# A shorter pause in a gather pipeline: GpSimd waits for three tiles of a quad, the fourth tile counts on a semaphore of its own

## The reference

```python
# network 0, three layers
agg = segment_sum(e_w[:, None] * h[src], dst)            # gather by src, sum by dst
h = layernorm(relu(agg / sum_w @ w_neigh.T + h @ w_root.T + b))
# network 1
ef = (relu(edge_attr @ We1 + be1) @ We2 + be2) * sigmoid(ts @ Wt + bt)
msg = relu(concat([x[row], ef]) @ Wn1 + bn1) @ Wn2 + bn2
x = x + segment_sum(msg, col)
# network 2, two layers: a matrix for each of 8 edge types
x = segment_sum(xt[src, etype8], dst) + x @ Wl + b
# network 3, two layers: 8 heads, 32 edge types
a = (kw[src, etype32] * q[dst]).sum(-1) * pri;  att = edge_softmax(a, dst)
h = segment_sum(v[src, etype32] * att, dst) ...
```

## Time and profile before

| | us |
|---|---|
| median of 3 runs | 6471.04 (6457.61 to 6473.24) |
| profiled execution, own time | 6410.16 |
| its span | 6408.1 |
| GpSimd busy in the span | 3221.9 (50%) |
| of that the gathers, line 479, 3128 of them | 3001.8 |
| TensorE matmul busy | 3293.9 (51%) |
| VectorE busy | 2162.9 (34%) |
| ScalarE busy | 1006.4 (16%) |
| mean granted TensorE clock | 0.652 of full speed |

### The profile page before, as it was taken

How to read it: one execution, slowest core, us unless ns; L and a number is a source line. 1 busy time by engine, 2 the same in 40 slices (tenths; PEclk the granted TensorE clock), 3 DMA queues, 4 the chain that set the end, 5 groups by cost and what they waited for, 6 DMA issues and landing times. The chain is left out here.

```text
span 6408.1 us, 51881 instructions
## 1 busy us (share of the span) xinstructions
PE 3293.9 (51%) x13857; PEld 2295.6 (36%) x13857; DVE 2162.9 (34%) x5075; ACT 1006.4 (16%) x2209; POOL 3221.9 (50%) x3406
## 2 busy tenths in 40 slices
PE   5554677767774555643463344643324356333263
PEld 3333455545552333332343232233324322333153
DVE  3222322232224222411121114533338544333485
ACT  0000322232222111200010002400004324000063
POOL 4665466546663666366646663046650320566403
PEclk7676777677776777755565556755557677555586
DMA  2111334333432332211131116976653579766453
GB/s 61 46 47 40 88 98 101 98 82 99 101 99 79 91 90 82 107 46 47 46 131 47 46 46 251 427 239 185 182 149 111 149 287 427 204 187 184 118 148 95
DMA packets 630965, 826.34 MB, mean 129 GB/s; under 512 B 93075, under 2 KB 510341, under 8 KB 618133
## 3 DMA queue, kind: packets, MB, share of 16 engines
q1 hardware_dynamic: 480117, 492.37, 22.9%
q0 software_dynamic: 120608, 276.12, 16.2%
q10 hardware_dynamic: 29952, 54.54, 2.9%
HBM read 470.63 MB, written 352.04 MB: 128 GB/s over the span
## 5 line engine op out<-in xcount | busy, mean ns | idle before, releaser
L479 POOL DMA_INDIRECT arena<-table,idx_s x3128 | 3001.8, 960 | 2353.5 <-issue 1095.5
L751 PE MATMUL ps<-arena,work 128*128 x4160 | 985.9, 378 | 1050.0 <-issue 934.9
L751 PEld LDWEIGHTS ps<-arena,work 128*128 128x128 f32 x4160 | 824.8, 274 | 1317.4 <-issue 1170.3
L1965 PE MATMUL ps<-arena,work 128*128 x1664 | 412.7, 426 | 693.7 <-issue 488.2
L1965 PEld LDWEIGHTS ps<-arena,work 128*128 128x128 f32 x1664 | 359.1, 317 | 748.6 <-issue 530.1
L459 DVE TENSOR_SCALAR work<-iota_row,dl_s,w_s 128x128 f32<-128x128 f32 x1248 | 350.4, 358 | 454.6 <-issue 349.4
L455 DVE TENSOR_TENSOR work<-ps,dl_s 128x512 f32<-128x512 f32 x208 | 143.8, 692 | 926.5 <-issue 617.0
L1934 DVE TENSOR_TENSOR arena<-arena,ps 128x128 f32<-128x128 f32 x832 | 182.7, 281 | 741.9 <-issue 500.0
L929 DVE SCALAR_TENSOR_TENSOR arena<-ps,vecs,arena 128x256 f32<-128x256 f32 x208 | 100.6, 484 | 893.9 <-issue 435.9
L1832 PE MATMUL ps<-arena,work 32*128 32x512 f32 x1600 | 299.1, 876 | 97.5 <-DVE work L1859 44.2
L510 PE MATMUL ps<-work,picks 128*104 128x512 f32 x416 | 313.4, 842 | 46.2 <-issue 42.8
(11 more groups left out here) (331 smaller groups left out, 3539.5 us busy)
## 6 DMA issues: line engine op xcount, KB each, us to landing
table<-arena SPq DMA_DIRECT2D x96, 2048.0 KB
onehot<-col_rows ACTq DMA_DIRECT2D x208, 256.0 KB
values<-arena SPq DMA_DIRECT2D x832, 64.0 KB
arena<-values SPq DMA_DIRECT2D x208, 256.0 KB
arena<-table,idx_s POOLq DMA_INDIRECT x3128
arena<-edge_times SPq DMA_DIRECT2D x208, 128.0 KB
edge_part<-arena SPq DMA_DIRECT2D x208, 128.0 KB
table<-arena SPq DMA_DIRECT2D x50, 512.0 KB
```

The costliest lines, as they stand in the source:

```text
L479: pool.indirect_dma_start(ring[:, ds(t % RING * 2 * H, width)], None, tab, bass.IndirectOffsetOnAxis(ap=idx_s[:, t:t + 1], axis=0)).then_i ...
L751: mm = pe.matmul(accf[:, ds(b, P)], o, arena[:, ds(slot, H)], start=False, stop=False, skip_group_check=True)
L1965: mm = pe.matmul(ps[:, n % 8, c * P:(c + 1) * P], across_ring[:, n % DEEP, c * P:(c + 1) * P], Qn_flat[:, ds(b, P)], start=True, stop=True)
```

## The change

`gathers` gets a second set of 16 semaphores, `fourth`. The fourth tile of a quad adds its 16 there, the other three add to `gathered` as before. `hand_over(k)` waits for 48 on the one and for 16 on the other. After each quad the quad before it is handed over, now always and only that one. Each `rest`-th quad GpSimd then waits for the three first tiles of the quad just issued, without a hand-over.

```diff
             def hand_over(k):
-                pool.wait_ge(gathered[k % U].sem, gathered[k % U].at(64 * (k // U) + 16 * min(4, EDGE_TILES - 4 * k)))
+                pool.wait_ge(gathered[k % U].sem, gathered[k % U].at(48 * (k // U) + 16 * min(3, EDGE_TILES - 4 * k)))
+                if 4 * k + 3 < EDGE_TILES:
+                    pool.wait_ge(fourth[k % U].sem, fourth[k % U].at(16 * (k // U) + 16))
...
                 pool.indirect_dma_start(ring[:, ds(t % RING * 2 * H, width)], None, tab,
-                                        bass.IndirectOffsetOnAxis(ap=idx_s[:, t:t + 1], axis=0)).then_inc(gathered[t // 4 % U].sem, 16)
+                                        bass.IndirectOffsetOnAxis(ap=idx_s[:, t:t + 1], axis=0)).then_inc((fourth if t % 4 == 3 else gathered)[t // 4 % U].sem, 16)
                 if t % 4 == 3:
-                    done = t // 4 + 1
-                    for k in range(handed[0], done if done % rest == 0 else done - 1):
-                        hand_over(k)
-                        handed[0] = k + 1
+                    k = t // 4
+                    if k > 0:
+                        hand_over(k - 1)
+                        handed[0] = k
+                    if (k + 1) % rest == 0:
+                        pool.wait_ge(gathered[k % U].sem, gathered[k % U].at(48 * (k // U) + 48))
             for k in range(handed[0], TILE_QUADS):
                 hand_over(k)
```

More of the change, by code:

```diff
@@ L182, in build @@
         gathered = [signal(f"gathered{u}") for u in range(U)]
+        fourth = [signal(f"fourth{u}") for u in range(U)]
         arrived = signal("arrived")
@@ L556, in gather_pass_over @@
             for k in range(TILE_QUADS):
-                gathered[k % U].base += 16 * min(4, EDGE_TILES - 4 * k)
+                gathered[k % U].base += 16 * min(3, EDGE_TILES - 4 * k)
+                fourth[k % U].base += 16 * (4 * k + 3 < EDGE_TILES)
         def fill_rows(pe, row):
@@ L1972, in score_phase @@
                 for q in range(TILE_QUADS):
-                    gathered[q % U].base += 16 * min(4, EDGE_TILES - 4 * q)
+                    gathered[q % U].base += 16 * min(3, EDGE_TILES - 4 * q)
+                    fourth[q % U].base += 16 * (4 * q + 3 < EDGE_TILES)
                 for s in row_in:
```

## The result

The changed kernel takes 6614.65 us (median of 4 runs, 6606.82 to 6622.54) against 6464.32 us (4 runs, 6445.94 to 6473.24) of the kernel before: ratio 1.0236, 95% interval 1.0209 to 1.0264. It is 150 us slower, where 253 us less were forecast.

What follows compares the result with a forecast made beforehand. GpSimd's row of gathers and rests was taken to bound 4580 of 6408 us. Savings of 96 (P2, P3), 75 (P1, P5, P6), 30 (P4) and 52 (P7, P8) sum to 253: 6471 - 253 = 6218 us, range 6150 to 6450.

Steps and rivals of the forecast that it cites:

- The view of the bound: GpSimd's gathers and rests set the length of all eight gather passes, 4580 of 6408 us.
- The 10 to 17 us over the rests: GpSimd's idle in P1, P4, P5 and P6 beyond its pace and rests, put down to waits for a full ring.
- those with one every 20 do: Argument for the rival: passes with a rest every 20 us show ring waits, those with one every 10 us none.
- the term 3 x (30 - 5) = 75 us: P1, P5, P6: 30 us saved at rests in each, less 5 for ring waits in TensorE's slow stretches; bounds 0 and 90.
- P2 and P3: 96 us gained was forecast: Consumer chain at 5.3 us a step makes each pass 551 us, 48 gained in place of 60; bounds 0 and 60.
- P4, P7 and P8: 82 us gained was forecast: Shorter rests save 30 us in P4 and 52 in P7 and P8 together, 1.1 at each of their rests.
- The size of a rest: Waiting for the third tile ends each of 240 rests 1.25 us earlier, 2.34 to 1.09: 300 us at GpSimd.
- The later hand-over: Quads at rests are handed over some 4 us later; taken as nothing, or 32 us if its cover goes.
- The Trainium skill's rule: DMA engines alternate queues by whole packets; if half the saving were lost, P7 and P8 give 30 us, not 52.
- The rival: TensorE's slow stretches come to P2 and P3, 152 us longer for both; net 70 slower, 6541 us, chance 0.17.
- in P1 rests don't stop a crawl either: Argument against the rival: one of TensorE's slow stretches in P1 has two rests inside it.

Runs made afterwards that it cites:

- The run with the full rest: Changed kernel with GpSimd also waiting for the fourth tile at each rest, hand-over still one quad late: 6481.52 us, ratio 1.0022 to the kernel before.
- the last set of runs: Kernel before with no rests and evenly paced gathers (1.53, 1.44 or 1.39 us by pass) in all passes: 6360.03 us against 6318.55 for the kernel before.

## Why the prediction was wrong

**The view of the bound failed.** The sentence "a pass lasts as long as GpSimd's row of gathers and rests" took the rests for the reason of the row's length. In P1, P5 and P6 they are not: P1's row was 553.5 us with full rests, 557.5 with short ones, 554.0 with none, and 558.7 at 1.31 us. There the consumers set the row already, at the speed that the gathers leave TensorE; GpSimd sets P1's only when it is slower still (575.6 us at 1.44, 592.1 with a full rest at every second quad). The 10 to 17 us over the rests, which I counted as a side matter, were this bound showing. (P4 doesn't belong in that list: 55.6 - 49 is 6.6 us, and it has no ring waits, so "those with one every 20 do" was misread too.) So the term 3 x (30 - 5) = 75 us failed, and the larger one of P2 and P3 below. I took a loss of 5 us in each of P1, P5 and P6 for the ring; it was all of the gain and more. GpSimd's idle over its pace ahead of quads that are no rest went from 12.1 to 32.2 us in P1, from 6.0 to 47.3 in P5 and from 10.9 to 44.9 in P6, against 15.3, 39.1 and 33.5 us that the rests themselves gave (50.5 to 35.2, 55.8 to 16.7, 50.5 to 17.0; P1's rests still hold ring waits).

**P2 and P3: 96 us gained was forecast, 98 lost was measured.** The chain was sized at 5.3 us from its free run of 4.97. That run was itself one under full rests. With the gathers denser the median step did fall, from 5.54 to 5.16 us, but 18 steps of P2 take 8 us and more, up to 43.7, where none did before, as TensorE's word to ScalarE comes up to 20 us late. The bounds, 0 to 60 us of gain, left out that the price of a step depends on GpSimd's rate.

**P4, P7 and P8: 82 us gained was forecast.** P4 lost 12 us, with 99 crawled matmuls where there were none; P7 and P8 lost 83 us in the profiles, of which by other kernels' tails some 40 to 60 are the lucky profile.

**The size of a rest** was right in kind and too small: in P1 it fell by 1.75 us and not by 1.25, as the third tile lands more than one pace ahead of the fourth. Were it so at all rests, 240 x 1.75 = 420 us would have been free at GpSimd; nothing of it arrived at the end of any pass.

**The later hand-over** was taken at nothing, 32 us if its cover goes. The run with the full rest has it alone: 0.2%, some 14 us.

**The Trainium skill's rule** on the turns of a DMA engine between its queues (DMA: Bandwidth & Descriptors, Queues, rings and completion order) was to speak for half a saving in P7 and P8. The rests there fell from a median of 3.5 and 3.7 us to 1.7 and 1.5, more than a whole pace, and over the 24 of each pass by 38 and 33 us where 26 was taken. So the lump that was to follow from the rule doesn't show; it didn't decide anything.

**The rival** that the crawl comes to P2 and P3 had 0.17 and 6541 us. It named the place, the coincidence of the earlier trace rows that gave it away, and the loss of the gain in P1, P5 and P6. Its 70 us were half of the loss. The argument against it, "in P1 rests don't stop a crawl either", was wrong: full rests at every fourth quad don't, but at every second they do, as the run with rest 2 in all passes shows. And it held the quiet time for the reason, where an even and slower pace does as well.

**What stays open**: what TensorE and the gathers share. It isn't the transfers at the moment they run, as TensorE crawls on for 6 us without any. Whether the bytes of a gather count isn't settled: P7 and P8 move twice as many and crawl less than P1 in the changed kernel, 36 and 37 against 121, but with five memsets at each rest P7 crawls more, 99 against 69. GpSimd's memsets don't matter; its own work for each gather wasn't told apart from the transfer. Whether it is the way of the completion signals, which each gather sends as TensorE does, was not tried. Each execution here has a span and a granted clock, so each was recorded in some form, and whether the recording has a part in it no run tells either. Nor is it known why the disturbance was weak in the last set of runs.

## What to carry to other kernels

A pause in a producer isn't waste because the consumers look idle beside it: before shortening it, ask whether other waits (a full ring) already take up part of any gain, and read those as a second bound and not as noise. Where the time of a pass doesn't follow the producer's pace in a small trial (one rest more, one less), the pace is a throttle that something else needs. The cheapest test is to put the same time in another form, here a memset ahead of each gather: it told apart "must be empty" from "must be slower", which no trace of the two kernels could. And compare the pace of the gathers between two waits, not the mean of a pass: a pass that waits for its consumers has a slow mean whatever the producer does.

## What the runs showed of the hardware that was not expected

- While GpSimd gathers 128 rows every 1.25 us, a matmul's signal reached ScalarE up to 20 us late (17.7 and 18.8 us in the rows above), and in other passes TensorE ran single matmuls some 2 us apart. At 1.44 us there was none of this in six passes, at 1.53 none in P2 and P3.
- It outlives the gathers: TensorE crawled until 6 us after the last one had landed, with no DMA packet in between, and began again 18.6 us after they had come back.
- The effect is graded: 112, 74, 67, 28 and 0 crawled matmuls in P1 at 1.25, 1.31, 1.34, 1.39 and 1.44 us.
- Five memsets in place of three at each rest, 3.0 us of pause and not 1.86, made the kernel 57 us faster though GpSimd did more.
- In P1 a wait for the third of four gathers was over 1.75 us before that for the fourth (0.59 us of idle in place of 2.34), with 1.25 us between their issues.
